# Two-layer transformer block, one core: the last two tiles ahead of the feed-forward next to last, and the output norm's roots a step later

## What is computed

```python
x = x + layernorm(mixer(layernorm(x)))
h0 = layernorm(x)                      # the input of layer 0
for l in range(2):                     # DEPTH = 2; two sequences of 1024 tokens
    h = shift_token(h0)                # channels 64..127 come from the token before
    q, k, v = split(h @ wqkv[l])       # 8 heads of 64
    q, k = rotary_xpos(l2norm(q) * q_scale, l2norm(k) * k_scale)
    h0 = h0 + local_attention(q, k, v) @ wo[l]       # windows of 64 tokens
    h = layernorm(shift_token(h0)) * ln_g + ln_b
    a, g = split(h @ w1[l] + b1[l])    # 341 hidden channels each
    h0 = h0 + (a * gelu(g)) @ w2[l] + b2[l]
out = x + layernorm(h0)                # the output norm
```

## Time and profile before

| | |
|---|---|
| runs | 462.72, 463.50, 463.67 us, median 463.5 |
| profiled execution | 463.3 us, its span 461.5 us |
| busy in the span | PE 359.1, DVE 336.4, POOL 298.0, ACT 280.5 us |
| mean granted clock of PE | 0.923 of full speed |

### The profile page before, as it was taken

The page is one execution under the profiler, slowest core; times in us unless marked ns, Lnnn a source line. Parts: engine busy times, 40 slices in busy tenths (PEclk is TensorE's granted clock), DMA queues, the critical chain, the costliest instruction groups (busy, mean ns, idle before and its releaser), DMA issues.

```text
span 461.5 us, 11300 instructions
## 1 busy us (share of the span) xinstructions
PE 359.1 (78%) x3832; PEld 294.3 (64%) x3832; DVE 336.4 (73%) x752; ACT 280.5 (61%) x844; POOL 298.0 (65%) x247
## 2 busy tenths in 40 slices
PE   2583076899998999899899979998949897678372
PEld 1362055687786878697778868886838776666251
DVE  6879954868778769868977897878766975754423
ACT  3352155867767867677767868767826774565020
POOL 2200439799999699969976994899477866540202
PEclk9996556999999999999999999999988999799857
DMA  8600131411431052115114320431015101110100
GB/s 272 184 0 0 34 112 39 121 36 31 110 82 30 2 154 57 28 50 134 36 25 112 78 56 1 132 81 31 7 33 144 42 15 28 45 30 3 23 22 23
DMA packets 42398, 28.21 MB, mean 61 GB/s; under 512 B 21699, under 2 KB 36597, under 8 KB 42357
## 3 DMA queue, kind: packets, MB, share of 16 engines
q1 hardware_dynamic: 42357, 27.68, 23.1%
HBM read 13.51 MB, written 3.15 MB: 36 GB/s over the span
## 4 chain that ended last, share of the span: by engine, by line
PE 45%; DVE 23%; POOL 12%; issue 9%; ACT 6%; DMA 2%; SPq 1%; DVEq 0%; POOLq 0%; ACTq 0%
DVE h L1088 5%; PE bank L725 5%; PE upper L664 5%; PE bank L682 5%; POOL rn L483 4%; DVE rot_sin L1064 3%; PE bank L548 3%; PE upper L637 3%; PE upper L643 3%; DVE rot_cos L1064 2%; ACT probs L841 2%; PE bank L608 2%; POOL rot L519 2%; PE bank L711 2%; PE bank L717 2%
## 5 line engine op out<-in xcount | busy, mean ns | idle before, releaser
L841 ACT ACTIVATE probs<-upper,neg_max 128x128 f32<-128x128 f32 x256 | 90.4, 368 | 62.1 <-DVE neg_max L1110 62.1
L483 POOL TENSOR_TENSOR rn<-floored,minus_half 128x16 f32<-128x16 f32 x32 | 93.7, 2929 | 2.7
L504 POOL TENSOR_TENSOR rot<-rot_cos,rot_sin 128x512 f32<-128x512 f32 x32 | 40.9, 1277 | 58.5 <-DVE rot_sin L1064 33.5
L519 POOL TENSOR_TENSOR rot<-rot,rn 128x1024 f32<-128x1024 f32 x32 | 60.9, 1902 | 1.9
L548 PE MATMUL bank<-wqkv_hi,act_t_hi 128*128 128x512 f32 x96 | 44.8, 467 | 21.4 <-DVE o_tok L1122 13.7
L1110 DVE TENSOR_REDUCE neg_max<-upper 128x4 f32<-128x512 f32 x64 | 43.0, 683 | 24.8 <-PE upper L664 24.7
L841 ACT ACTIVATION_READ_ACCUMULATOR probs<-upper,neg_max 128x1 f32 x256 | 52.8, 206 | 0.0
L1064 DVE TENSOR_TENSOR rot_cos<-bank,tab 128x512 f32<-128x512 f32 x64 | 43.6, 681 | 2.9 <-PE bank L552 2.9
L1064 DVE TENSOR_TENSOR rot_sin<-bank,tab 128x512 f32<-128x512 f32 x64 | 43.4, 679 | 0.0
L548 PEld LDWEIGHTS bank<-wqkv_hi,act_t_hi 128*128 128x128 f32 x96 | 19.2, 200 | 36.2 <-issue 23.6
L505 POOL TENSOR_TENSOR rot<-rot_cos,rot_sin 128x512 f32<-128x512 f32 x32 | 40.9, 1277 | 0.0
(11 more groups left out here) (128 smaller groups left out, 886.3 us busy)
## 6 DMA issues: line engine op xcount, KB each, us to landing
v_mid<-v_tok SPq DMA_DIRECT2D x64, 128.0 KB, 2.3
tab_raw<-tables SPq DMA_DIRECT2D x8, 512.0 KB, 3.3
h_tok<-group_in SPq DMA_DIRECT2D x14, 128.0 KB, 3.4
x_res<-group_in SPq DMA_DIRECT2D x28, 64.0 KB, 1.8
wqkv_raw<-wqkv SPq DMA_DIRECT2D x2, 768.0 KB, 6.7
x_in<-x SPq DMA_DIRECT2D x4, 256.0 KB, 3.5
head_scale<-head_scales SPq DMA_DIRECT2D x8, 128.0 KB, 4.0
group_in<-normed SPq DMA_DIRECT2D x4, 256.0 KB
```

Source lines behind the costliest of these rows:

```text
L483: pool.tensor_tensor(rn[:, 0:2 * HEADS], floored[:, 0:2 * HEADS], minus_half[:, :], ALU.pow).then_inc(rn_ready, 1)
L504: pool.tensor_tensor(rot[cur.par][:, :, 0:32], rot_cos[:, :, 0:32], rot_sin[:, :, 32:64], ALU.add).then_inc(rot_added, 1)
L519: pool.tensor_tensor(rot[cur.par][:, :, :], rot[cur.par][:, :, :], rn[:, 0:2 * HEADS].unsqueeze(2).broadcast_to([P, 2 * HEADS, DH]), ALU.m ...
L841: last = act.activation(probs[:, h, :], s_bank[half][:, (h % 4) * P:(h % 4 + 1) * P], ACT.Exp, bias=neg_max[a.par][:, h:h + 1], accum_out= ...
```

## The change

It does three things.

1. **Ending.** body(7) stops after its steps 0 and 1, and body(8) is gone. Each engine has an `ending()` in their place: tiles 30 and 31 go through `wo` and the residual before or inside feed-forward 6. Tile 31's transposes go to `pt_bank[0]` and its projection to `pt_bank[1]`, put between the two halves of the first chunk of feed-forward 6 (`between`). The last group's residual sums go to a buffer of their own, `x_last` (the memory of `normed`), so `load_h2(7)` needs no free `x_attn`, and DVE takes the variances of `h2` for group 7 before it sums group 6.
2. **Output norm.** The variances of `y` stay in step 3. POOL's roots move from step 3 to step 0 of the next body, behind the scaling of `rot`; DVE's rows of `y_out` move to the end of that step 0, POOL's add to step 1, and SP's store to step 2.
3. **Passes.** The second layer's loop over G = 5 and 6 is written out as two bodies.

The core of the diff:

```diff
+        x_last = normed
@@ passes
-            for layer in range(DEPTH):
+            for layer in range(DEPTH - 1):
...
+            for G in range(GROUPS * (DEPTH - 1) + 1, LAST - 1):
+                body(G, DEPTH - 1)
+            body(LAST - 1, DEPTH - 1, 2)
+            ending()
@@ sync
+                src = x_attn
+                if isinstance(F, int) and F == LAST - 1:
+                    need(sp, h2t_done, F)
+                    need(sp, carry_in, 16 * F)
+                    src = x_last
...
+            def ending():
+                store(LAST - 3, DEPTH - 1)
+                load_h2(LAST - 1)
+                store(LAST - 2, DEPTH - 1)
+                store(LAST - 1, DEPTH - 1)
@@ gpsimd
-                    if j == 3 and (G > GROUPS if number else layer == DEPTH - 1):
-                        deviation_roots(G - GROUPS, y_var, y_floored, y_dev)
                     if cur.valid:
...
+                    if j == 0 and number and G > GROUPS + 1:
+                        deviation_roots(G - 1 - GROUPS, y_var, y_floored, y_dev)
+                    if j == 1 and number and G > GROUPS + 1:
+                        add_input(G - 2 - GROUPS)
@@ tensor
+            def ending():
+                third, last = tile(DEPTH * TILES - 2), tile(DEPTH * TILES - 1)
+                project_out(tile(DEPTH * TILES - 3))
+                transpose_probs(last, 0)
+                transpose_probs(last, 1)
+                transpose_o(third)
+                mix_values(last)
+                transpose_h2(LAST - 2)
+                project_out(third)
+                transpose_o(last, pt_bank[0])
+                feed_forward(LAST - 2, DEPTH - 1, DEPTH * TILES + 3, lambda: project_out(last, pt_bank[1]))
+                pe.wait_ge(y_read, LAST)
+                transpose_h2(LAST - 1)
+                feed_forward(LAST - 1, DEPTH - 1, DEPTH * TILES + 4)
@@ scalar
+            def ending():
...
+                save_probs(last)
+                save_o(third)
+                save_h2(LAST - 2, DEPTH - 1, h2_hi)
+                save_o(last, pt_bank[0])
+                save_h2(LAST - 2, DEPTH - 1, h2_t)
+                gelus(LAST - 2, DEPTH - 1)
...
@@ vector
                     if final:
                         variances(y, y_var)
-                        need(dve, stored, FIRST_LAYER + 16 * (G - 1 - GROUPS))
-                        normalise_tiles(y_out, y, y_dev, G - GROUPS).then_inc(y_normed, 1)
                     if j == 0 and not (number and not 0 <= G < LAST - 1):
                         split_inputs(G + 1)
+                    if j == 0 and number and G > GROUPS + 1:
+                        normalise_out(G - 2 - GROUPS)
```

More of the change, by code:

```diff
@@ L405, in _, with body @@
             sp.wait_ge(xf_stored, 16 * (2 * GROUPS - 1))
-            def body(G, layer):
+            def body(G, layer, count=GT):
                 number = isinstance(G, int)
-                for j in range(GT):
+                for j in range(count):
                     cur = At(G, j, 0, layer)
@@ L490, in deviation_roots, with add_input, body @@
                 pool.tensor_tensor(rn[:, 2 * HEADS:], floored[:, 2 * HEADS:], minus_half[:, 0:GT], ALU.pow).then_inc(done, 1)
+            def add_input(g):
+                pool.wait_ge(y_normed, g + 1)
+                pool.tensor_tensor(y_out[:, :, :], y_out[:, :, :], group_tiles(x_in, g), ALU.add).then_inc(out_ready, 1)
             pool.wait_ge(init_done, 5)
-            def body(G, layer):
+            def body(G, layer, count=GT):
                 number = isinstance(G, int)
-                for j in range(GT):
+                for j in range(count):
                     cur = At(G, j, 0, layer)
@@ L532, in body @@
                             pool.tensor_copy(k_t[:, :, 0:WINDOW], k_t[:, :, GTOK:GTOK + WINDOW]).then_inc(k_carried, 1)
[L533 to L538, removed]
+                    if j == 0 and number and G > GROUPS + 1:
[3 more added lines that the diff above has]
+            def ending():
+                deviation_roots(LAST, h2_var, h2_floored, h2_dev)
+                for g in (GROUPS - 2, GROUPS - 1):
+                    deviation_roots(g + 1, y_var, y_floored, y_dev)
+                    add_input(g)
+            passes(pool, body, ending)
         W_IN = 16 * DEPTH * 12
@@ L876, in body @@
                     if done.valid:
[L877 to L879 removed]
+                        save_o(done)
                     if j == 0 and not (number and not 0 <= G < LAST - 1):
@@ L884, in body, with ending @@
                         l = F // GROUPS if number else layer
-                        act.wait_ge(h2t_done, F + 1)
                         for dst in (h2_hi, h2_t):
[L887 to L894, removed]
+                            save_h2(F, l, dst)
+                        gelus(F, l)
+            def ending():
+                third, last = tile(DEPTH * TILES - 2), tile(DEPTH * TILES - 1)
+                exponentials(last, 0)
+                exponentials(last, 1)
+                save_probs(last)
[4 more added lines that the diff above has]
+                gelus(LAST - 2, DEPTH - 1)
+                for dst in (h2_hi, h2_t):
+                    save_h2(LAST - 1, DEPTH - 1, dst)
+                gelus(LAST - 1, DEPTH - 1)
+            passes(act, body, ending)
         @block.vector
```

130 lines of the change are left out of this document (93 added, 37 removed).

## The result

The changed kernel takes 456.06 us (median of 4 runs, 454.93 to 456.89) against 463.56 us for the kernel before (462.72 to 463.67). The ratio is 0.984, with a 95% interval of 0.981 to 0.986. The forecast was 452.5 us in a range of 448.0 to 458.0: the direction and the range held, and 3.6 us of the expected 11.1 did not come. The four runs of the changed kernel spread by 2.0 us, the four of the kernel before by 1.0; later batches of the kernel before, of 7 and 13 runs, spread by 1.3 to 2.5.

The account below looks back on a forecast made before the run. The prediction took the first layer as PE-bound, the second as losing time to the output-norm stall and the ending. From the 461.5 us span, -11.2 (ending) +0.4 (stalls) gave 450.7, plus 1.8 for 452.5 us; own range 449.5-455, wider 448.0-458.0.

Parts of the forecast that it names:

- The stall in step 3 goes: Second layer, sum `y` of group 4 to `neg_max`: 7.6 us instead of 13.9, removing a 6.3 us stall.
- It comes back in step 0: End of step 0, bodies 6 and 7: DVE waits again for POOL's roots; new stall 6.4 us in body(6).
- The clock behind it: PE at 1.2 GHz after each moved stall in bodies 6 and 7: 1.9 us each, bounds 0 to 3.4.
- POOL's add at 0 (0 to 1.3): POOL's add in step 1 may meet DVE's rows of `h`: cost taken as 0, bounds 0 to 1.3 us.
- Feed-forward 6 longer by 1.2: PE's added projections and transposes ahead of or inside feed-forward 6 delay it 1.2 us, bounds 0.6 to 2.2.
- The last `h` 8.6 us earlier: Ending: rows of the last `h` start at 430.9 instead of 439.5, with the DMAs hidden behind DVE's gates.
- The last feed-forward at 2.4 GHz: Feed-forward 7 keeps full clock after a PE gap of 2 to 3 us, saving the whole 2.64 us.
- Rival B: The last feed-forward stays at 1.2 GHz, its 2.6 us gain does not come: 455.1 us, chance 0.18.
- Written-out passes: Writing out the second layer's loop over groups costs 0 us, bounds -0.4 to +0.4.
- D: Both moved stalls pay 3.4 us for clock, rows meet POOL at 1.3 each: +5.6, 458 us, chance 0.12.

Follow-up runs that it names:

- e3: The changed kernel with DVE's rows of `y_out` moved to step 1, behind its `ss`, POOL's roots unmoved: 442.46 us, ratio 0.955 to the kernel before.
- e6: The changed kernel with POOL's output-norm roots at the head of step 0, DVE's rows left at its end: 441.17 us, ratio 0.950 to the kernel before.
- e4: The changed kernel with 20 identity transposes on PE between feed-forward 6 and the transposes of the last `h`: 453.48 us, ratio 0.981 to the kernel before.
- e5: The changed kernel with POOL's add moved to step 2 (group 5's into `ending()`) and the store to step 3: 454.00 us, ratio 0.979.
- e2: The kernel before with only the second layer's loop written out: 463.27 us, ratio 0.999 to the kernel before.
- e7: The changed kernel with the edits of e3, e4 and e5 together: 439.05 us, ratio 0.947 to the kernel before.
- e8: e7 plus identity transposes on PE where it waits for ACT ahead of the probability transposes of tiles 30 and 31: 437.61 us, ratio 0.943.
- e10: e8 with POOL's output-norm roots at the head of step 0, DVE's rows still in step 1: 438.49 us, ratio 0.945 to the kernel before.
- e9: e8 with tile 31's projection between the first and second chunks of feed-forward 6, and ACT saving `h_t` ahead of `o_t`: 439.41 us, ratio 0.947.

## Why the prediction was right or wrong, point by point

Against the sum, the span came out at 453.9 instead of 450.7: 3.2 us. One reading of the rows was wrong and changed nothing: the four rows of `y_out` of before did not end with POOL's scaling of `rot` at 342.2, but at 343.0 (340.35 + 2.68), 0.8 us behind it.

1. **The stall in step 3 goes: right.** 7.5 us from sum 4 to `neg_max` instead of 13.9; forecast 7.6.
2. **It comes back in step 0: right, in size too.** In body(6) `neg_max` was forecast at 309.0 on the first layer's clock, which is 352.3 on this one's; it came at 352.0. In body(7) it came 404.30 - 382.07 = 22.2 us after the sum; forecast 22.5. e3 and e6 show the cause by taking it away from either side.
3. **The clock behind it: right where it was expected.** The terms were 1.9 us each. From `neg_max` to the rows of `h` it took 15.2 us in body(6), against 13.4 before and in the first layer (302.56 to 315.95), so 1.8; in body(7) it took 15.2 against 13.1, so 2.1. Not foreseen was a second stretch in body(6), 371.4 to 374.7. It cost 1.2 us (14.9 us from the rows of `h` to the sum, against 13.7 in e4 with the same rows and the same wait), and since e4's trace has none, it is partly chance that it stands in this sum.
4. **POOL's add at 0 (0 to 1.3): the wrong end was taken.** The reason given, that the rows of `h` and POOL already take turns there, was true but did not bound it: one operation more in the queue was one more turn. The rows took 4.34 us, 0.6 more than the 3.75 of before, and 1.0 more than without the add (3.38 in e5). That is inside the bounds. The Trainium skill (GPSIMD Engine Reference, 1. Specifications) has the two engines share their SBUF interfaces, with contention when the Vector instruction is in a 2-port mode or has two SBUF inputs. The prediction weighed that for the rows of `y_out`, which met nothing of POOL (1.11 us) until e3 put them beside it (2.50 us). For the rows of `h` the trace agrees with contention, at 1.0 us for one more operation of 1.27. In which mode the rows ran, no trace shows.
5. **Feed-forward 6 longer by 1.2: right.** 430.97 - 419.46 = 11.5 us from rows of `h` to sum, against 10.33.
6. **The last `h` 8.6 us earlier: the mechanism was right.** Rows of `h` 6 to rows of `h` 7 took 13.05 us against 21.8 before, 8.7 less; no wait for the DMAs.
7. **The last feed-forward at 2.4 GHz: wrong.** This is the largest miss. The step that failed is "only its gaps of 6 us and more are followed by 1.2 GHz in these rows". PE had been idle for 2.84 us, then worked 1.09 and waited 0.87 for `h_hi`, and the clock was 0.50 from 432.8 to 439.6. The trace of before had no gap between 2 and 6 us at such a place, so its silence was no evidence. Rival B had 0.18; it is what happened, though 1.8 us (12.2 against 10.33) and not 2.6 were lost, since the low stretch ended inside. e4 and the eight other traces named there show it.
8. **Written-out passes: right** (e2).

So the last feed-forward (1.8 us) and body(6) (1.5 instead of 0.1) make up nearly all of the 3.2 us. In body(6) that is 0.6 for the add and 1.2 for the second low stretch, less the 0.3 us by which `neg_max` came early. The measured 456.06 us lies 3.6 us above the forecast, outside the forecast's own 449.5 to 455, and 1.0 us above rival B. The wider range held because it had the price of B and most of D in it; that part of D's price came, as a low stretch at another place than D named, is luck.

## What to carry to other kernels

An instruction that waits for another engine costs its own engine everything queued behind it, so a step moved "one later" has to be set against the place of its producer: here both moved together, and the wait moved with them. Moving only one of the two, either the reader later (e3) or the producer's 1.3 us of work earlier (e6), was worth 13.6 and 14.9 us. When idle time on PE is cut but not closed, put a price on the low clock behind what remains, and if it stands at the end of a chain, cheap work in the gap gave it back here (e4).

## What the runs showed of the hardware that was not expected

A wait of 2.83 or 2.84 us on PE ahead of the last `h`, then 0.6 to 1.1 us of transposes and another wait of 0.87, was followed by 1.2 GHz in all five kernels that have it. With 20 transposes in the gap it was not, in e4, e7, e8 and e10, though in e9 a gap of 1.49 us behind the same 20 transposes was followed by a low stretch of 3.4 us. The length of one wait does not decide it alone: a wait of 2.27 us in body(6), behind the same instructions, was followed by 1.2 GHz in the kernel after and not in e4.

Runs of one kernel spread by 2.0 us (kernel after), 4.3 (e4) and 0.4 (e8). Filling the gaps does not explain that: e10 has all the fillers of e8 and spreads by 2.2 us, and e5 and e6, with their gap open, by 0.9 and 0.8. That the spread comes from where the low stretches fall would fit the pair of traces in body(6), but was not shown: only one execution of each kernel has a trace.
